# Row maxima of two cross attentions from the high halves alone, two heads to a pass, and a new order of work on TensorE

## What is computed

```
# attention 1
scores = einsum('bhtd,bhsd->bhts', Q, K) * scale          # Q [4,16,512,32], K [4,16,1601,32]
attn   = softmax(where(mask, scores, -inf), axis=-1)
out    = einsum('bhts,bhsd->bhtd', attn, V)
# attention 3
attn = einsum('bkhd,bnhd->bhkn', q, kmat) / DH            # q [4,16,512,32], kmat [4,16,2113,32]
attn = softmax(where(full_mask, attn, -inf), axis=-1)
attn_out = einsum('bhkn,bnhd->bkhd', attn, v)
```

## Time and profile before

| | us |
|---|---|
| median of 3 runs | 5259.54 |
| lowest, highest | 5256.17, 5262.85 |
| the profiled execution, its time | 5261.2 |
| span of its trace | 5259.4 |
| mean granted TensorE clock in it | 0.945 |

### The profile page before, as it was taken

How to read it: one execution, slowest core, us unless ns; L and a number is a source line. 1 busy time by engine, 2 the same in 40 slices (tenths; PEclk the granted TensorE clock), 3 DMA queues, 4 the chain that set the end, 5 groups by cost and what they waited for, 6 DMA issues and landing times. The chain is left out here.

```text
span 5259.4 us, 76538 instructions
## 1 busy us (share of the span) xinstructions
PE 4670.2 (89%) x29250; PEld 1681.2 (32%) x29250; DVE 3684.5 (70%) x4667; ACT 3029.1 (58%) x5554; POOL 2161.0 (41%) x977
## 2 busy tenths in 40 slices
PE   7978998987686999997899999996789999995999
PEld 2323433443232233332222222222333333331444
DVE  6749989997563877770699999993567777771421
ACT  5644344443552566663488888885436666665432
POOL 1226666665333578873000000000008888885000
PEclk9989999999797899998999999998889999998999
DMA  3353433434112333313111111112434232312100
GB/s 130 127 169 102 113 106 105 116 110 120 68 57 64 74 70 70 70 45 124 57 33 33 33 33 33 33 29 71 119 96 84 63 78 59 75 34 77 65 24 17
DMA packets 474871, 391.97 MB, mean 75 GB/s; under 512 B 175151, under 2 KB 372628, under 8 KB 474472
## 3 DMA queue, kind: packets, MB, share of 16 engines
q1 hardware_dynamic: 474496, 387.00, 26.9%
HBM read 246.50 MB, written 139.34 MB: 73 GB/s over the span
## 5 line engine op out<-in xcount | busy, mean ns | idle before, releaser
L3114 DVE TENSOR_REDUCE att_part<-att_scores 128x2 f32<-128x802 f32 x1024 | 953.3, 986 | 105.8 <-PE att_scores L2953 94.0
L3087 ACT ACTIVATE att_prob<-att_lower 128x512 f32<-128x512 f32 (+1 forms) x1664 | 882.8, 597 | 125.2 <-PE att_lower L2967 103.9
L3921 DVE TENSOR_REDUCE att_part<-att_scores 128x1 f32<-128x423 f32 x1280 | 675.9, 589 | 219.5 <-PE att_scores L3624 219.5
L3865 ACT ACTIVATE att_prob<-att_lower 128x512 f32<-128x512 f32 (+1 forms) x1088 | 563.4, 603 | 244.0 <-PE att_lower L3636 242.1
L3905 POOL TENSOR_TENSOR att_acc<-att_acc,att_prob 128x1024 f32<-128x1024 f32 (+2 forms) x240 | 671.2, 2797 | 52.1 <-ACT att_prob L3865 23.0
L2690 DVE TENSOR_REDUCE att_part<-att_scores 128x1 f32<-128x401 f32 x1024 | 515.7, 567 | 162.8 <-PE att_scores L2504 162.7
L1684 POOL TENSOR_TENSOR scan_z<-scan_r,scan_states 128x512 f32<-128x512 f32 x256 | 467.7, 1831 | 344.3 <-DVE scan_states L1761 337.4
L2629 ACT ACTIVATE att_prob<-att_scores 128x512 f32<-128x512 f32 (+1 forms) x832 | 431.1, 602 | 196.5 <-PE att_scores L2516 196.5
L2982 PE MATMUL att_lower<-att_prob,att_v 128*32 128x256 f32 (+1 forms) x6144 | 520.9, 411 | 19.7 <-issue 19.7
L3101 POOL TENSOR_TENSOR att_out<-att_sums_sb,att_spread 128x512 f32<-128x512 f32 x32 | 40.7, 1272 | 1163.0 <-DMA att_spread<-recips 1163.0
L2670 POOL TENSOR_TENSOR att_acc<-att_acc,att_prob 128x1024 f32<-128x1024 f32 (+2 forms) x176 | 449.8, 2555 | 69.5 <-ACT att_prob L2629 57.4
(11 more groups left out here) (485 smaller groups left out, 8197.3 us busy)
## 6 DMA issues: line engine op xcount, KB each, us to landing
v<-scan_val SPq DMA_DIRECT2D x96, 256.0 KB, 2.3
att_v<-v SPq DMA_DIRECT2D x32, 768.0 KB
att_spread<-recips SPq DMA_DIRECT2D x64, 256.0 KB
mix_plane<-in_mask SPq DMA_DIRECT2D x16, 800.5 KB, 8.1
att_k<-k1hi SPq DMA_DIRECT2D x32, 400.2 KB
att_k<-k3hi SPq DMA_DIRECT2D x32, 400.2 KB
scan_x<-in_ctx_t SPq DMA_DIRECT2D x12, 1024.0 KB, 5.5
o<-att_out SPq DMA_DIRECT2D x32, 256.0 KB
```

The costliest lines, as they stand in the source:

```text
L3087: nc.scalar.activation(prob[g % NP][0:kw(kt), h, :], scores2[0:kw(kt), n % RING2, :], ACT.Exp).then_inc(exped, 1)
L3114: nc.vector.reduce_max(part[q % 2][:, :, ec, piece], scores1[:, bank["unit", p], :, 0:PIECE], AX.X).then_inc(reduced, 1)
L3865: nc.scalar.activation(prob[g % NP][0:kw(kt), h, :], scores2[0:kw(kt), n % RING2, :], ACT.Exp).then_inc(exped, 1)
L3921: nc.vector.reduce_max(part[q % 2][:, hc, piece:piece + 1], scores1[:, bank["piece", p], 0:PIECE], AX.X).then_inc(reduced, 1)
```

## The change

In both attentions:

- Pass 1 uses the high halves alone. New tiles `QP` and `KP` hold two heads, one on rows 0 to 31 and one on rows 64 to 95, with constant and mask on rows 32 and 96. A **unit** is one piece for two heads: two matmuls over 33 rows each, at rows 0 and 64 of the array, into two banks, and one reduction on VectorE over both. There are 32 units per block in attention 1 and 40 in attention 3, where there were 64 and 80 pieces. Pass 2 has all three products as before, so the maximum subtracted is one of slightly rounded scores; softmax doesn't depend on it.
- The ring of pass 1 becomes two units (four banks). The ring of shifts becomes two banks: shift n now waits for exponential n-2.
- A group on TensorE becomes: shifts 0 and 1, a unit if due, mix, a unit if due, shifts 2 and 3, count if due, a unit if due (`SLOTS` = 3, `units_by(g, slot)`).
- `NB` becomes 2: Q and K are loaded one block ahead. The new tiles are loaded by `load_pieces`, six DMAs (eight in attention 3), as soon as pass 1 has left the buffer, and come first at the start of attention 1. TensorE waits for the full Q and K only at the first shift of a block.
- The branches of `cross_attention` for layer 3, which nothing calls, are removed.

The diff of `cross_attention`, cut to its core; `latents_and_attention` has the same, with `units_at` in the dense part.

```
-    UNITS = QUAD * C * PIECES
-    RING1, RING2, NB, NP = 3, 3, 4, 5
-    LEAD, TURN, LAG = 5, 6, 2
+    SIDES, EACH = 2, QUAD // 2
+    UNITS = EACH * C * PIECES
+    RING1, RING2, NB, NP = 2, 2, 2, 5
+    LEAD, TURN, LAG = 5, 3, 2
+    SLOTS = 3
...
-    def pieces_by(g):
-        return min(N * UNITS, AHEAD + (g + 1) * UNITS // NT)
+    def units_by(g, slot=SLOTS - 1):
+        return min(N * UNITS, AHEAD + (g * SLOTS + slot + 1) * UNITS // (NT * SLOTS))
...
+        QP = [ph.sb(f"qp{i}", [P, EACH, T], F16) for i in range(2)]
+        KP = [ph.sb(f"kp{i}", [P, EACH, NK], F16) for i in range(2)]
...
-        scores1 = ph.ps("scores1", [P, RING1, T])
+        scores1 = ph.ps("scores1", [P, RING1, SIDES, T])
...
+                def load_pieces(s):
+                    i = s % 2
+                    rows = slice(s * P, (s + 1) * P)
+                    for a in range(SIDES):
+                        r, m = slice(64 * a, 64 * a + dh), slice(64 * a + dh, 64 * a + dh + 1)
+                        sp.dma_start(QP[i][r], w[f"q{layer}hi"][rows].rearrange("(e a d) t -> a d e t", a=SIDES, d=dh)[a]).then_inc(ploaded[i], 16)
+                        sp.dma_start(KP[i][r], w[f"k{layer}hi"][rows].rearrange("(e a d) t -> a d e t", a=SIDES, d=dh)[a]).then_inc(ploaded[i], 16)
+                        sp.dma_start(KP[i][m], w[f"km{layer}"][s // C, 0:EACH].unsqueeze(0)).then_inc(ploaded[i], 16)
...
                 for s in range(N):
                     if s:
-                        if s + 3 < N:
+                        if s + 1 < N:
                             sp.wait_ge(shifted, s * NT * QUAD)
-                            load_keys(s + 3)
-                        if s + 1 < N:
+                            load_keys(s + 1)
...
                         send_top(s + 1)
+                    if s + 3 < N:
+                        sp.wait_ge(scored, (s + 2) * UNITS)
+                        load_pieces(s + 3)
...
-                        b = take(("piece", p), reduced, p + 1)
-                        nc.tensor.matmul(scores1[:, b, 0:PIECE], Q[i][0:TOP, h, c * P:(c + 1) * P], K[i][0:TOP, h, k0:k0 + PIECE],
-                                         start=True, stop=True).then_inc(scored, 1)
+                        b = take(("unit", p), reduced, p + 1)
+                        for a in range(SIDES):
+                            r = slice(64 * a, 64 * a + dh + 1)
+                            ins = nc.tensor.matmul(scores1[:, b, a, 0:PIECE], QP[i][r, e, c * P:(c + 1) * P], KP[i][r, e, k0:k0 + PIECE],
+                                                   start=True, stop=True)
+                        ins.then_inc(scored, 1)
...
                     if g < G:
                         if kt == 0:
+                            if s < NB:
+                                pe.wait_ge(fixed[s], 16 * 2)
+                            pe.wait_ge(loaded[s % NB], 16 * LOADS * (s // NB + 1))
                             pe.wait_ge(topsent[s % 2], 16 * (s // 2 + 1))
-                        for h in range(QUAD):
-                            shift(s, kt, h)
-                            if issued < pieces_by(g):
-                                next(one)
-                                issued += 1
+                        shift(s, kt, 0)
+                        shift(s, kt, 1)
+                        units(units_by(g, 0))
                     if g >= LAG:
                         ms, mk = divmod(g - LAG, NT)
                         mix(ms, mk)
-                        if mk in counts_at:
-                            count(ms, counts_at[mk])
-                    while g < G and issued < pieces_by(g):
-                        next(one)
-                        issued += 1
+                    if g < G:
+                        units(units_by(g, 1))
+                        shift(s, kt, 2)
+                        shift(s, kt, 3)
+                    if g >= LAG and mk in counts_at:
+                        count(ms, counts_at[mk])
+                    if g < G:
+                        units(units_by(g, 2))
...
-                    nc.vector.reduce_max(part[q % 2][:, hc, piece:piece + 1], scores1[:, bank["piece", p], 0:PIECE], AX.X).then_inc(reduced, 1)
+                    pair = part[q % 2][:].rearrange("p (e a c) k -> p e a c k", e=EACH, a=SIDES)[:, e, :, c, piece]
+                    nc.vector.reduce_max(pair, scores1[:, bank["unit", p], :, 0:PIECE], AX.X).then_inc(reduced, 1)
```

More of the change, by code:

```diff
@@ L3670, in _, with units @@
                 issued = j = 0
+                def units(upto):
+                    nonlocal issued
+                    while issued < upto:
+                        next(one)
+                        issued += 1
                 def group(pairs):
-                    nonlocal issued, j
+                    nonlocal j
                     if j >= RING0:
@@ L3678, in group @@
                     ins.then_inc(product, 1)
-                    while issued < pieces_at(j):
-                        next(one)
-                        issued += 1
+                    units(units_at(j))
                     j += 1
```

233 lines of the change are left out of this document (127 added, 106 removed).

## The result

| | before | after |
|---|---|---|
| median of the runs, us | 5257.90 (4 runs, 5256.17 to 5262.85) | 5382.11 (4 runs, 5373.46 to 5383.72) |
| ratio, with 95% interval | | 1.0231 [1.0214, 1.0249] |
| span of the profiled execution, mean granted clock | 5259.4, 0.945 | 5381.9, 0.945 |

The change makes the kernel 2.3% slower. The forecast was 5422 us with a range of 5310 to 5480; the time lies 40 us under the forecast and within the range.

The account below looks back on a forecast made before the run. TensorE was taken to bound both attentions (99.88 of 100 us busy). Terms of +71 (attention 1), +99 (attention 3) and -8 (start) gave +162 us on 5261.2, or 5423, stated as 5422 us; range 5310 to 5480.

Parts of the forecast that it names:

- the theory: Attentions 1 and 3: two shift banks make TensorE wait, and units' changes of shape eat what their columns save.
- The ring's turn-round: Shifts of both attentions: a bank is occupied 1.15 us; third shift to next group's second takes 1.64 us.
- The walk: One group stepped through on TensorE: 2.95 us without units, 3.55 with both beside the mix, against 2.84 before.
- A change of shape: TensorE switching between 98-row products, 33-row units and 32-column strips: 0.12 us each, ends 0 and 0.15.
- The count's price: Groups with a count and a unit in the third slot: 2.04 us replaces 1.64, 0.40 more.
- The start: Start of attention 1: first unit 7 us after first load instead of 15.3, so -8 us, ends -5 and -11.
- The stretches between: Last blocks: +2.4 us in attention 1, +3.5 in attention 3; dense part of attention 3: 0, ends -9 and +5.
- TensorE stays the bound: Rival: banks return early enough that no shift waits; faster, 5087 us with free changes too; chance 0.09.
- Free changes: Rival: changes of shape cost nothing, units beside a mix 0.18 us, blocks 44.2 and 57.6, time 5320; chance 0.13.
- No wait, but changes at 0.12: Rival: blocks of 43.1 and 55.1 us, time 5261, so the change moves nothing; chance 0.05.
- The rival of the falling clock: Rival: TensorE's waits in each group lower the granted clock, 22% of time at 1.2 GHz, 5560 us; chance 0.04.
- the halves of a pair run one behind the other: Rival: a unit's two matmuls don't overlap beside full-array products, 0.175 us more per unit, 5556 us; chance 0.03.

Follow-up runs that it names:

- the kernel with moved units: Kernel after with the units, and in some groups the mix, placed elsewhere, mostly where shifts wait for an exponential: 5307.05 us, 1.0094 of before.
- The run without counts: Kernel after with the matmuls of count() left out, shifts still on two banks: 5337.45 us.
- the full-height run: Kernel after with each unit's 33-row pair replaced by two 97-row matmuls of half as many columns: 5310.11 us beside 5259.8.
- the bank runs: Kernel before with two shift banks instead of three: 5464.31 us beside 5259.8; kernel after without counts, den's bank given to the shifts: 5167.8 against 5337.45.
- the three kernels without counts: Kernel after without count() matmuls: two shift banks 5337.45 us; three banks 5167.8; three banks and units at full height 5148.77.

## Why the prediction was right, and where its sizes were off

- **The sign and the mechanism held.** TensorE has idle time that exponentials end, at the first two shifts of a group; VectorE is idle for 32 of 100 us, waiting for units; the granted clock is 1.00 in the running blocks. Both halves of the theory are shown: the ring by taking a bank away (5.8 and 7.1 us a block dearer) and by giving one back (7.2 cheaper in attention 3), the changes by removing them (2.5 and 3.2 cheaper).
- **The size was off by a quarter.** The forecast was +162 us on the profiled execution, the trace shows +122.5. The points below name the terms; nearly all of them err to the same side.
- **The ring's turn-round was sized 0.08 too long.** The walk had 1.64 us from the third shift to the next group's second, from 0.51 to the exponential, 0.64 to the free bank and 0.49 between two. The rows show 0.42, 0.65 and 0.49, so 1.56. The 0.51 came from the earlier trace rows. Traces of this study hold both values (0.51 from 2107.47 to 2107.98 in the kernel with moved units), and what makes the difference stays open.
- **A change of shape was sized 0.12 and is 0.10** between shift and unit, and 0.09 to 0.10 from a unit into the mix. The way out of the mix was not taken apart: its 1.00 us to the next product is the same in every kernel here. Four changes lie in the 1.91 us beside the mix, which measured 1.87. Together the two make the group 3.43 for 3.55, and blocks 46.4 and 59.6 for 47.3 and 61.4. That is the step that failed in size: over fifteen blocks +62 us for +69 in attention 1 and +77 for +96 in attention 3, where 17 groups a block carry the error.
- **The count's price held.** From one third shift to the next, with a count, a unit behind it and another behind the mix, the walk gives 3.65 (2.04, and 1.61 with one unit beside the mix).

```profile
2100.44 0.62 PE L2536 MATMUL att_scores<-att_q,att_k 98*65 98x512 f16 x2
2100.99 1.06 PE L2557 MATMUL att_den<-att_prob,const_ones 128*32 128x512 f32 x8
...
2104.08 0.61 PE L2536 MATMUL att_scores<-att_q,att_k 98*128 98x512 f16 x2
```

  The rows have 3.64. A count partly fills time in which TensorE would wait. The run without counts confirms it: removing 4.3 us of TensorE's work per block of attention 1 shortened the undisturbed block by 2.0 only.
- **The start was sized -8 and is -12.7**, of which the first unit's earlier start is 9.9. I took 7 us from first load to first unit where it is 5.4, and gave nothing for the shorter advance (39.9 us in place of 42.4), because I priced a unit's reduction at 0.93 to 0.98 where two pieces cost 0.964; in the advance the units stand 0.91 apart (39.9 / 44).
- **The stretches between gave less than nothing.** From attention 1's last block to attention 3's first, -5.7 for the +2.4 of the last block and 0 in the dense part; behind attention 3's last first addition +0.1 for +3.5. No run took these apart, so their cause stays open.
- **Two things were not in the walk.** Units wait for their own banks, also two now; of the 88.8 us of idle weight loads in 500 most lies behind a running mix or count, and TensorE's own idle time for it is 5.0. And the first blocks of both attentions last 48.79 and 63.45 us in place of 46.41 and 59.62, which partly cancels the errors above. Stretches at half clock lie there:

```profile
1740.00:1760.00 20.00, 18.75 (x102) 4.04 (x104) 12.65 (x13) 11.97 (x23) 14.02 (x6) 0.88 0.00 1
3970.00:3990.00 20.00, 11.90 (x42) 2.24 (x40) 10.21 (x13) 7.68 (x13) 4.51 (x1) 0.60 0.67 168
```

  But in before the clock is low at the start as well (0.84 from 1740 to 1760), and its first blocks, 40.21 and 53.37, are shorter than the others. So the clock is at most a part of it, and the rest stays open.

- **The rivals.** "TensorE stays the bound" fell with every wait. Free changes fell with the full-height run. "No wait, but changes at 0.12" gave 5261 and fell with the bank runs. The rival of the falling clock was wrong for after's running blocks; the three kernels without counts show such falls in attention 1. In "TensorE stays the bound" a sum doesn't come out: the saved columns, 5.4 and 7.0 us, make blocks of 37.3 and 48.0 and not 38.0 and 48.7, so 21 us less than 5087. It changes no verdict. That the halves of a pair run one behind the other is out as well: the next instruction starts 0.27 behind a unit, less than the 0.35 of two pieces in series.

## What to carry to other kernels

Price a change that saves columns with everything that it takes: here 32 units saved 5.6 us of columns in a block, brought 64 changes (6.4 us by the 0.10 of the timeline, an estimate, of which 2.5 lengthened the block and waits covered the rest), and took a bank out of a ring whose turn-round (shift to exponential to free bank) was 1.07 us. The bank was the dearest part (5.8 us a block by itself). The Trainium skill (TensorEngine Tiling (Array Packing), Gotcha 1: PSUM Pressure) says that different row tiles write to different banks; that is why a pair needs two, and why the question "which ring pays for it" belongs ahead of the first line of code.

If a ring is too short, put the work that is free to move, and all its changes of shape, into the wait, and leave the long instruction by itself: that order gave back 75 us here. And before a larger rebuild look at what the engines wait for at a stage's start: some lines there made the kernel 0.3% faster.

## What the runs showed of the hardware

- A change between a 98-row and a 33-row product costs 0.10 us of TensorE each way (0.53 against 0.43 there, 0.27 against 0.17 back). Into the strips of 32 columns it is about as much: the mix stands 0.27 behind a unit or a piece.
- The granted clock fell in kernels that were only a little less busy than after. In the kernel without counts and with two banks TensorE was busy for 90% of attention 1, and the granted clock fell to 0.50 (1.2 GHz) for some 17 us in three blocks of sixteen, each 6 us longer for it, while after, at 94%, kept 1.00 through its running blocks. The busy share alone doesn't tell: the kernel with units at full height and two banks kept 1.00 at 92%, and the kernel without counts kept it at 90% in attention 3. Some 7 us ahead of the second and the third of these falls TensorE had stood for 1.38 and 1.18 us at a block's first shift; ahead of the first fall it had not. What sets it off I can't tell from these runs.
- The small transfer of the row maxima takes 6.0 to 6.8 us from issue to landing (eleven of them in after, from 1816 to 2281). In the kernels without counts TensorE stood for it at a block's first shift, by up to 3.50 us. Short blocks alone don't bring this: with blocks of 43.95 and units at full height there is no such stop, with 44.39 and no counts there is.
